# A routed-expert stage with one load queue split in two, and three smaller moves of order

## The chip, the cores and the metric

The kernel runs on one core of one Trainium2 chip. The metric is the device time of one execution in microseconds (us). Below, TensorE is the matrix engine (PE in the rows), VectorE is DVE, ScalarE is ACT, GpSimd is POOL and SyncE is SP; SP only waits and issues transfers.

## The reference, cut to what matters

Sixteen sequences of 64 rows (1024 rows in all, 512 wide) pass through three blocks, each added to its input:

```
x = x + cross_attention(layernorm(x), ctx)        # 16 heads, 1601 context rows per sequence
x = x + linear_attention(layernorm(x))            # elu + 1 feature maps, 16 heads
x = x + experts(layernorm(x))                     # 8 experts, each row goes to its best 2
experts: logits = x @ router.T; p = softmax(logits); two best experts of each row
         h = x @ w1[e].T (2048 wide); y = h[1024:] * silu(h[:1024]); out += p_e * (y @ w2[e].T)
```

## The kernel before, in words

All weights and activations that matter are held as two float32r parts: ScalarE rounds a tile to its high part, and VectorE or GpSimd subtracts to get the low part. A product is then three matmuls (high-high, high-low, low-high).

**The head.** The function `cross_attention` opens with the projections of the first sequence's context, `copy_unit` 0, 1, 2 and so on: TensorE fills one of two PSUM banks (L719), ScalarE copies it out (L617, L621). TensorE may fill a bank again when the copy of two units earlier is done. Units 0 to 3 make keys, units 4 and 5 are the first that need the value weights: for these ScalarE rounds `wv_hi` (L666) and VectorE subtracts `wv_lo` (L548). In the kernel before, ScalarE rounds `wv_hi` ahead of its copy of unit 0. ScalarE's square root before the copy of unit 6 (L674) waits for the variances of all rows of x.

**Linear attention and routing.** In `attend_route_and_experts` a loop over t works as a pipeline on tiles of 128 rows: at step t, tile t-1 makes its key-value blocks (KV, L1789), t-2 its heads (HEADS, L1811), t-3 is transposed (ATT_T, L1827), t-4 is projected (PROJ, L1836), then VectorE's `start_rows` (x, stats, mean, std: L1584, L902 to L904), a square root on ScalarE (L1393), VectorE's `finish_rows` (rstd, xn: L893, L894), the transpose of tile t-5 (TURN, L1848) and routing of tile t-6. Routing a tile is a chain: `route` on TensorE (logits, L1733), `choose` on VectorE (L1590 to L1600), `rank` on TensorE (L1745, L1747), `assign` on VectorE (L1606 to L1610), after which GpSimd scatters the tile's rows into `rows_in` (L1278). `route` of a tile waits for `assign` of the tile before it. Steps 8 to 13 have no new tile to start; there, `choose` and `assign` of tile t-6 stand at the end of VectorE's step and `rank` at the end of TensorE's. After them VectorE makes the tables (`slot_tables`, `combine_places`, `combine_weights`), in one row of small instructions.

**The experts.** `over_slots` runs a slot for each block of up to 384 rows of one expert, in order of falling counts: slots 0 to 6, written out, with WIDTH 384 (slots 0 to 4), 342 and 292 columns, then two kinds inside a loop that runs as often as the counts ask (not at all with these inputs) and a last slot of 256 columns. A slot has IT = 8 steps u. In step u TensorE does `up(s, u)` (24 matmuls, L1707), `down_part` of the slot before (9 matmuls, L1721) and in steps 3, 4 and 5 the transposes of one tile of the next slot's rows (`turn_rows`, 4 matmuls, L1691). The second and third `turn_rows` wait for VectorE's `rest_rows` (L1431) of the tile before, which follows ScalarE's `silu` (L1362), VectorE's product y (L1548) and ScalarE's `round_rows` (L1329) of the same step.

First-layer weights (w1) come in eight pieces of 512 KB a slot into RAW = 4 buffers. ScalarE's `split_w1` (L1309) and VectorE's (L1421) for piece u+2 (AHEAD = 2) stand in step u. Second-layer weights (w2) come in four pieces of 512 KB into two buffers; ScalarE's `split_w2` (L1316) of piece c stands in step 2(c+1), and GpSimd subtracts its low part (L1261), which frees the buffer. The last piece of a slot is split in step 0 of the next.

All these loads are issued by SP, in one order written by hand; a wait in it holds back everything behind it:

```python
for u in range(IT):
    ...                                   # slot 0, u == RAW: wait for the scatter, load_rows(0)
    if u == IT // 2 and not last:
        load_rows(s + 1)                  # the rows of the next slot, 768 KB
    sp.wait_ge(w1_lo_done, n - RAW + 1)   # then w1 piece u (L1235)
    if u % WC == WC - 1:
        sp.wait_ge(w2_lo_done, k - 1)     # then w2 piece u // 2 (L1242)
```

So the load of w2 piece 1 of a slot waits for GpSimd's work on the last piece of the slot before (step 0), piece 2 for step 2 and piece 3 for step 4, with the w1 pieces 4 to 7 standing behind them. ScalarE already issues one transfer a slot, `store_down` (L1339).

Of the kernel before, what the change touches and what calls it, by code (L numbers as in the profile page):

```python
# [118 lines left out]
def cross_attention(nc, ident, x, ctx, wq, bq, wk, wv, bk, bv, q_parts, attn_t, inv_t, rows_in, rows_out):  # L119
# [4 lines left out]
    with ExitStack() as mem:  # L124
# [480 lines left out]
        def _(act):  # L605
# [59 lines left out]
            act.wait_ge(wv_loaded, 16)  # L665
            nc.scalar.copy(wv_hi[:], wv_raw).then_inc(w_hi_done, 1)  # L666
            act.wait_ge(zeroed, 5)
            act.wait_ge(bias_loaded, 48)
            for kind, k in start_steps():
                if kind == "unit":  # L670
# [364 lines left out]
def attend_route_and_experts(nc, ident, m, rows_in, rows_out, w1, w2, out):  # L1035
# [4 lines left out]
    with ExitStack() as mem:  # L1040
# [142 lines left out]
        STEPS = TT + ROUTE  # L1183
# [26 lines left out]
        def _(sp):  # L1210
# [9 lines left out]
            def slot(s, par, last, width):  # L1220
# [3 lines left out]
                for u in range(IT):  # L1224
                    n = IT * s + u
                    if u == RAW and is_first(s):

                        sp.wait_ge(dispatched, 16 * 2 * TT)
                        sp.wait_ge(tables_done, 2)
                        load_rows(0)  # L1230
# [6 lines left out]
                    if u % WC == WC - 1:  # L1237
                        c = u // WC
                        k = NW2 * s + c
                        if positive(k - 1):  # L1240
                            sp.wait_ge(w2_lo_done, k - 1)
                        sp.dma_start(w2_raw[c % 2][:], w2[bass.ds(e, 1), c].rearrange(  # L1242
                            "a p (k n) -> (a p) k n", k=WC)).then_inc(w2_loaded[c % 2], 16)
# [58 lines left out]
        def _(act):  # L1302
# [7 lines left out]

            def split_w2(s, c):

                act.wait_ge(w2_loaded[c % 2], 16 * (s * (NW2 // 2) + c // 2 + 1))
                if positive(s):
                    act.wait_ge(parts_done, IT * (s - 1) + WC * (c + 1))
                nc.scalar.copy(w2_hi[:, WC * c:WC * c + WC, :], w2_raw[c % 2][:]).then_inc(w2_hi_done, 1)  # L1316
# [25 lines left out]
            def slot(s, par, last, width):  # L1342
                first = is_first(s)
                for u in range(IT):
# [17 lines left out]
                    nc.scalar.activation(silu[u % 2][:, 0:width], ps_up[u % 2][:, 0, 0:width], ACT.Silu).then_inc(silu_done, 1)  # L1362
                    if TURN_ROWS < u <= TURN_ROWS + RB and not last:
                        round_rows(s + 1, 1 - par, u - TURN_ROWS - 1)
# [45 lines left out]
        def _(dve):  # L1410
# [202 lines left out]
            for t in range(STEPS):  # L1613
                if 0 <= t - TURN < TT:
                    finish_rows(nc, dve, m, t - TURN, then, norm_sems)
                if ROUTE <= t < TT:
                    choose(t - ROUTE)
                r = t - KV
# [26 lines left out]
                if ROUTE <= t < TT:  # L1645
                    assign(t - ROUTE)
                r = t - PROJ
                if 0 <= r < TT:
                    start_rows(nc, dve, m, r, ready, then, norm_sems)
                if t >= TT:  # L1650
                    choose(t - ROUTE)
                    assign(t - ROUTE)
# [22 lines left out]
        def _(pe):  # L1675
# [95 lines left out]
            for t in range(STEPS):  # L1771
# [47 lines left out]
                if 0 <= r < TT:  # L1819
# [9 lines left out]
                    last.then_inc(att_turned, 1)  # L1829
                r = t - PROJ  # L1830
# [8 lines left out]
                if t >= TT:  # L1839
# [11 lines left out]
                if t >= TT:  # L1851
                    rank(t)
# [51 lines left out]
```

## Time and profile before

| | |
|---|---|
| three runs | 2516.23, 2516.41, 2518.18 us (median 2516.41) |
| the profiled execution | 2518.01 us, of which the profile's span is 2516.3 us |
| granted TensorE clock, mean | 0.974 |
| busy, TensorE / VectorE / ScalarE / GpSimd | 94% / 52% / 43% / 43% |
| cross attention | from 0 to about 1850 us, TensorE busy nearly throughout |
| linear attention and routing | about 1894 to 2060 us |
| experts, eight slots | 2078 to about 2491 us |
| gather, weighing, output | to 2516.3 us |

A row of the timeline gives start, duration, engine, line, operation, the tiles written and read, the count, and in square brackets the engine's idle time just before and who ended it. The chain of waits is the path followed back from the last instruction; its rows give start, duration and what ran or was waited for.

### The profile page before, as it was taken

Reading aid. Unit: us, or ns where it says so; the run is one execution under the profiler, and the core shown is the slowest. Engines: PE = TensorE matmul, PEld = TensorE weight load, DVE = VectorE, ACT = ScalarE, POOL = GpSimd, SP = SyncE. Lnnn points to the kernel's source line nnn. Section 1 sums busy time; section 2 is a strip of 40 time slices with the busy share of each in tenths; the row PEclk is TensorE's granted clock in tenths of the full one; section 3 lists DMA queues with packets and bytes.
Section 4 is the critical chain, followed back from the end, with each engine's and each line's share of the span. In section 5 each row is a group of like instructions: output and inputs, shape, how many; then the busy total and the mean of one; then the engine's idle time right before and its main releaser. Section 6 shows DMA issues by size and latency. Waiting matters only on the chain. (4 is left out here: it accounts for less than half of the span.)

```text
span 2516.3 us, 41241 instructions
## 1 busy us (share of the span) xinstructions
PE 2366.8 (94%) x14585; PEld 2092.1 (83%) x14585; DVE 1296.1 (52%) x2185; ACT 1086.3 (43%) x1865; POOL 1076.6 (43%) x439
## 2 busy tenths in 40 slices
PE   8999999999999999999999999999658958999985
PEld 7798998889899889989988998988527738999875
DVE  3245555555455555555545555555654465555544
ACT  3354544445444444444545454544412214444432
POOL 2255555555555555555555555555520021111114
PEclk9999999999999999999999999999879979999998
DMA  4311121221112121111212111123040034444444
GB/s 154 104 41 47 45 60 41 62 56 41 48 45 59 41 65 52 41 48 45 65 37 70 47 41 48 45 74 99 7 159 1 18 113 143 151 151 151 141 149 155
DMA packets 150050, 186.13 MB, mean 74 GB/s; under 512 B 79552, under 2 KB 108224, under 8 KB 149824
## 3 DMA queue, kind: packets, MB, share of 16 engines
q1 hardware_dynamic: 144192, 168.76, 21.7%
q0 software_dynamic: 2560, 8.39, 1.0%
q10 hardware_dynamic: 3072, 6.03, 0.6%
q8 instruction: 134, 2.20, 0.4%
q14 instruction: 92, 0.75, 0.2%
HBM read 139.29 MB, written 43.84 MB: 73 GB/s over the span
## 5 line engine op out<-in xcount | busy, mean ns | idle before, releaser
L399 POOL TENSOR_TENSOR k_parts<-k_t,k_parts 64x1602 fp32r<-64x1602 f32 x128 | 426.1, 3329 | 448.9 <-DVE k_parts L464 448.8
L719 PE MATMUL ps_kv<-ctx_hi,wk_hi 128*128 128x256 f32 (+1 forms) x1536 | 463.3, 302 | 9.1 <-DVE ctx_lo L578 7.6
L719 PE MATMUL ps_kv<-ctx_lo,wk_hi 128*128 128x256 f32 (+1 forms) x1536 | 441.2, 287 | 0.0
L719 PE MATMUL ps_kv<-ctx_hi,wk_lo 128*128 128x256 f32 (+1 forms) x1536 | 441.1, 287 | 0.0
L510 DVE TENSOR_TENSOR probs_t<-ps_pt,probs_t 128x512 fp32r<-128x512 f32 x368 | 205.9, 559 | 445.9 <-ACT probs_t L629 443.6
L413 POOL TENSOR_TENSOR v_parts<-v,v_parts 128x832 fp32r<-128x832 f32 x128 | 283.3, 2213 | 335.3 <-ACT v_parts L647 333.8
L719 PE MATMUL ps_kv<-wv_hi,ctx_hi 128*128 128x512 f32 (+1 forms) x832 | 340.9, 410 | 0.0
L719 PE MATMUL ps_kv<-wv_hi,ctx_lo 128*128 128x512 f32 (+1 forms) x832 | 327.9, 394 | 0.0
L719 PE MATMUL ps_kv<-wv_lo,ctx_hi 128*128 128x512 f32 (+1 forms) x832 | 327.1, 393 | 0.0
L617 ACT ACTIVATE k_t<-ps_kv,bk_sb 128x256 f32<-128x256 f32 (+1 forms) x384 | 185.6, 484 | 310.9 <-PE ps_kv L719 307.5
L719 PEld LDWEIGHTS ps_kv<-ctx_hi,wk_hi 128*128 128x128 f32 x1536 | 292.0, 190 | 12.5 <-issue 10.0
L719 PEld LDWEIGHTS ps_kv<-ctx_lo,wk_hi 128*128 128x128 f32 x1536 | 292.2, 190 | 1.9 <-issue 1.2
L719 PEld LDWEIGHTS ps_kv<-ctx_hi,wk_lo 128*128 128x128 f32 x1536 | 290.5, 189 | 0.0
L637 ACT ACTIVATE probs_both<-ps_s,neg_max 128x1601 f32<-128x1601 f32 x128 | 204.9, 1601 | 194.1 <-DVE neg_max L496 194.1
L388 POOL TENSOR_TENSOR ctx_lo<-ctx_raw,ctx_hi 128x1024 fp32r<-128x1024 f32 (+1 forms) x96 | 238.8, 2487 | 87.0 <-DVE ctx_hi L453 87.0
L494 DVE TENSOR_REDUCE row_max<-ps_s 128x1 f32<-128x1601 f32 x128 | 233.6, 1825 | 26.9 <-PE ps_s L733 19.3
L629 ACT CAST probs_t<-ps_pt 128x512 fp32r<-128x512 f32 x368 | 177.3, 482 | 161.4 <-PE ps_pt L765 152.2
L745 PEld LDWEIGHTS ps_o<-probs_t,v_parts 128*128 128x128 f32 (+1 forms) x1664 | 215.3, 191 | 30.1 <-DVE probs_t L510 20.0
L745 PE MATMUL ps_o<-probs_t,v_parts 128*128 128x256 f32 (+1 forms) x1664 | 220.4, 284 | 17.8 <-DVE probs_t L510 17.8
L621 ACT COPY v<-ps_kv 128x512 f32<-128x512 f32 (+1 forms) x208 | 120.7, 580 | 249.1 <-PE ps_kv L719 249.1
L1261 POOL TENSOR_TENSOR w_lo<-w_raw,w_hi 128x1024 fp32r<-128x1024 f32 x32 | 78.9, 2464 | 345.6 <-ACT w_hi L1316 345.6
L733 PE MATMUL ps_s<-k_parts,q_blocks 128*128 128x512 f32 (+2 forms) x1024 | 218.4, 356 | 2.0 <-issue 1.3
(275 smaller groups left out, 4113.4 us busy)
## 6 DMA issues: line engine op xcount, KB each, us to landing
w_raw<-w_dram SPq DMA_DIRECT2D x96, 512.0 KB, 4.9
ctx_raw<-ctx_dram SPq DMA_DIRECT2D x81, 512.0 KB, 3.9
rows_in<-zeros SPq DMA_DIRECT2D x150, 128.0 KB, 3.6
ctx_raw<-ctx_dram SPq DMA_DIRECT2D x16, 644.0 KB, 5.6
q_blocks<-q_parts SPq DMA_DIRECT2D x256, 32.0 KB, 1.9
rows<-rows_in SPq DMA_DIRECT2D x8, 768.0 KB, 6.2
rows_out<-zeros SPq DMA_DIRECT2D x1, 5376.0 KB, 17.7
rows_out<-down ACTq DMA_DIRECT2D x7, 768.0 KB, 3.6
```

Of the source, the lines that this page charges most:

```text
L388: nc.gpsimd.tensor_tensor(ctx_lo[c % 2][:, 0:w], ctx_raw[c % 2][:, 0:w], ctx_hi[c % 2][:, 0:w].bitcast(F32), ALU.subtract).then_inc(ctx_lo ...
L399: nc.gpsimd.tensor_tensor(k_parts[64 - 64 * s:128 - 64 * s, :], k_t[par][64 * s:64 * s + 64, g, :], k_parts[64 * s:64 * s + 64, :].bitcast ...
L413: nc.gpsimd.tensor_tensor(v_parts[:, :, 1, :], v[par][:, :, 64 * p:64 * p + 64], v_parts[:, :, 0, :].bitcast(F32), ALU.subtract).then_inc( ...
L494: nc.vector.tensor_reduce(row_max[:, q:q + 1], ps_s[:, S0:S0 + LC], AX.X, ALU.max).then_inc(max_done, 1)
L510: nc.vector.tensor_tensor(probs_t[0:m, j:j + k, 1, :], ps_turned[kv][g][0:m, 0:k, :], probs_t[0:m, j:j + k, 0, :].bitcast(F32), ALU.subtra ...
L617: nc.scalar.activation(k_t[par][:, which, CW * c:CW * c + w], ps_kv[bank][:, 0:w], ACT.Identity, bias=bk_sb[:, which:which + 1]).then_inc( ...
L621: nc.scalar.copy(v[par][0:m, which, :], ps_kv[bank][0:m, :]).then_inc(kv_copied, 1)
L629: nc.scalar.copy(probs_t[0:m, j:j + k, 0, :], ps_turned[kv][g][0:m, 0:k, :]).then_inc(pt_hi_done, 1)
L637: nc.scalar.activation(probs[q], ps_s[:, S0:S0 + LC], ACT.Exp, bias=neg_max[:, q:q + 1], scale=SCALE, accum_out=row_sum[:, q:q + 1]).then_ ...
L719: last = nc.tensor.matmul(o, still, moving, start=(k == 0 and i == 0), stop=(k == DT - 1 and i == 2))
L733: last = nc.tensor.matmul(ps_s[:, c0:c1], q_blocks[half][:, p % 4, part, :], k_parts[:, c0 - S0:c1 - S0], start=(part == 0), stop=(part == 1))
L745: last = nc.tensor.matmul(ps_o[:, 0:2], v_parts[0:m, j, :, :].rearrange("p a b -> p (a b)"), probs_t[0:m, j, :, :], start=(j == 0), stop=( ...
```

## The change

Four edits. (1) The w2 loads leave SP's order and are issued by ScalarE, through a new function `load_w2`: piece 0 after `silu` of step 0, piece 1 after that of step 1, piece 2 after step 3, piece 3 after step 5, each with the same wait for GpSimd as before; ScalarE reads the slot's expert number from the table once a slot. (2) In slot 0 SP issues the load of the first rows, with its wait for the scatter, ahead of w1 piece 2 (u == AHEAD) instead of ahead of piece 4. (3) For tiles 2 to 7 `choose`, `rank` and `assign` move from the end of step t to step t+1: `choose` after `finish_rows`, `rank` ahead of PROJ, `assign` after the heads and ahead of `start_rows`; the loop gets one step more. (4) ScalarE copies units 0 and 1 out before it rounds the value weights.

```diff
-            act.wait_ge(wv_loaded, 16)
-            nc.scalar.copy(wv_hi[:], wv_raw).then_inc(w_hi_done, 1)
             act.wait_ge(zeroed, 5)
             act.wait_ge(bias_loaded, 48)
             for kind, k in start_steps():
+                if kind == "unit" and k == 2:
+                    act.wait_ge(wv_loaded, 16)
+                    nc.scalar.copy(wv_hi[:], wv_raw).then_inc(w_hi_done, 1)
...
-        STEPS = TT + ROUTE
+        STEPS = TT + ROUTE + 1
...
-                    if u == RAW and is_first(s):
+                    if u == AHEAD and is_first(s):
...
-                    if u % WC == WC - 1:
-                        c = u // WC
-                        k = NW2 * s + c
-                        if positive(k - 1):
-                            sp.wait_ge(w2_lo_done, k - 1)
-                        sp.dma_start(w2_raw[c % 2][:], w2[bass.ds(e, 1), c].rearrange(
-                            "a p (k n) -> (a p) k n", k=WC)).then_inc(w2_loaded[c % 2], 16)
...
+            def load_w2(s, e, c):
+
+                k = NW2 * s + c
+                if positive(k - 1):
+                    act.wait_ge(w2_lo_done, k - 1)
+                act.dma_start(w2_raw[c % 2][:], w2[bass.ds(e, 1), c].rearrange(
+                    "a p (k n) -> (a p) k n", k=WC)).then_inc(w2_loaded[c % 2], 16)
...
+                    if u == 0:
+                        if first:
+                            act.wait_ge(tables_done, 1)
+                        e = act.value_load(slot_expert[0:1, bass.ds(s, 1)], min_val=0, max_val=E - 1)
+                        load_w2(s, e, 0)
+                    if u % WC == WC - 1 and u // WC + 1 < NW2:
+                        load_w2(s, e, u // WC + 1)
...
+                if t > TT:
+                    choose(t - 1 - ROUTE)
...
+                elif t > TT:
+                    assign(t - 1 - ROUTE)
...
-                if t >= TT:
-                    choose(t - ROUTE)
-                    assign(t - ROUTE)
...
+                if t > TT:
+                    rank(t - 1)
                 r = t - PROJ
...
-                if t >= TT:
+                if TT <= t < TT + ROUTE:
                     route(t, TT)
...
-                if t >= TT:
-                    rank(t)
```

## Rows read from the trace of the kernel before

**Rows 1.** TensorE's waits, 2040 us to the end: us in total, times, longest.

```profile
PE ps_one L1691 <- DVE rows_lo L1431: 13.1, 6, 4.6
```

**Rows 2.** SP's waits from 2060 us; the landing times of its 64 w1 loads (L1235).

```profile
SPq L1242 <- POOL w_lo L1261: 327.0, 30, 17.2
```

```profile
DMA to landing us min/median/max: 3.1/5.6/8.7
```

**Rows 3.** The chain of waits, slots 5 and 6.

```profile
2369.37 0.44 PE ps_one L1691 x4
...
2375.67 3.79 PE ps_pair L1707 x24
2379.45 2.06 PE ps_one L1721 x9
...
2388.73 0.33 SPq L1242
...
2390.45 8.00 DMA w_raw<-w_dram
```

**Rows 4.** Timeline of ScalarE, slots 1 to 6: ends of slots, two steps.

```profile
2173.45 1.56 ACT L1337 COPY down<-ps_one 128x512 f32<-128x512 f32 x3 [1.59 <-PE ps_one L1721]
...
2278.11 1.56 ACT L1337 COPY down<-ps_one 128x512 f32<-128x512 f32 x3 [1.59 <-PE ps_one L1721]
...
2329.65 1.56 ACT L1337 COPY down<-ps_one 128x512 f32<-128x512 f32 x3 [1.59 <-PE ps_one L1721]
...
2381.53 1.57 ACT L1337 COPY down<-ps_one 128x512 f32<-128x512 f32 x3 [1.58 <-PE ps_one L1721]
...
2426.33 0.41 ACT L1362 ACTIVATE silu<-ps_pair 128x292 f32<-128x292 f32 x1 [2.20 <-PE ps_pair L1707]
...
2431.61 0.42 ACT L1362 ACTIVATE silu<-ps_pair 128x292 f32<-128x292 f32 x1 [2.70 <-PE ps_pair L1707]
...
2433.70 1.56 ACT L1337 COPY down<-ps_one 128x512 f32<-128x512 f32 x3 [1.67 <-PE ps_one L1721]
```

**Rows 5.** Timeline of TensorE in slot 0.

```profile
2104.80 0.66 PE L1691 MATMUL ps_one<-ident,rows 128*128 128x128 f32 x4 [3.32 <-DVE rows_lo L1431]
```

**Rows 6.** Start of the experts: SP's timeline, chain of waits, timeline of VectorE.

```profile
2060.70 0.89 SPq L1235 DMA_DIRECT2D w_raw<-w_dram  x2
```

```profile
2064.57 9.22 DMA rows<-rows_in
```

```profile
2074.43 0.19 DVE L1535 TENSOR_REDUCE weight<-cross 128x16 f32<-128x32 f32 x1
2075.61 0.69 DVE L1431 TENSOR_TENSOR rows_lo<-ps_one,rows_hi 128x512 fp32r<-128x512 f32 x1 [0.99 <-ACT rows_hi L1329]
```

**Rows 7.** Timeline of TensorE, then VectorE, routing steps 7 to 9.

```profile
2018.53 0.95 PE L1733 MATMUL ps_one<-router_sb,o_t 128*128 128x8 f32 x8
...
2021.87 0.24 PE L1745 MATMUL ps_one<-chosen,before 128*128 128x8 f32 x1 [1.89 <-DVE chosen L1597]
...
2024.20 3.60 PE L1836 MATMUL ps_one<-lwo_sb,att_t 128*128 128x512 f32 x8
```

```profile
2012.30 0.16 DVE L893 RECIPROCAL rstd<-std 128x1 f32<-128x1 f32 x1 [0.27 <-ACT std L1393]
2012.50 0.55 DVE L894 TENSOR_SCALAR xn<-x,mean_var,rstd 128x512 f32<-128x512 f32 x1
...
2020.41 0.15 DVE L904 TENSOR_SCALAR std<-mean_var 128x1 f32<-128x1 f32 x1
```

**Rows 8.** Timeline of the head, all engines.

```profile
11.59 1.90 ACT L666 CAST wv_hi<-probs_both 128x2048 fp32r<-128x2048 f32 x1 [2.13 <-DMA probs_both<-wv_dram]
...
13.52 2.29 DVE L548 TENSOR_TENSOR wv_lo<-probs_both,wv_hi 128x2048 fp32r<-128x2048 f32 x1 [3.33 <-ACT wv_hi L666]
...
14.01 0.36 PE L719 MATMUL ps_kv<-ctx_hi,wk_hi 128*128 128x256 f32 x1 [0.98 <-ACT k_t L617]
...
16.95 0.39 PE L719 MATMUL ps_kv<-wv_hi,ctx_hi 128*128 128x512 f32 x1
...
26.08 0.39 PE L719 MATMUL ps_kv<-ctx_hi,wk_hi 128*128 128x256 f32 x1 [0.58 <-ACT k_t L617]
```

## The prediction

> **What bounds the kernel now.** The page's part 2 shows TensorE busy nine tenths or more from the second slice to past 1850 us; no edit but the fourth touches anything before that, and the fourth stands in its first 30 us. So I read TensorE's waits in the last 480 us and, for the experts, what stands behind them. The largest repeated wait is for `rest_rows`, 13.1 us in six pieces [rows 1]. The reader is to see that this is not VectorE's own slowness: the chain of waits leads from it back through ScalarE's `split_w1` to a w1 load that took 8.00 us, and in front of that stands SP at L1242, the w2 load [rows 3]. SP's own waits say why: 327.0 us, 30 times, it stood at L1242 for GpSimd's low part, at worst 17.2 us [rows 2]. The w1 load behind it needed a buffer that had been free long before. So in the experts TensorE is bound by its own work in some slots and by late issue of w1 in others.
>
> How much that costs is read from the ends of slots [rows 4]. Slot 4 took 2329.65 - 2278.11 = 51.5 us, which is TensorE's own work and no stall. Slots 2 and 3, of the same width, took 104.66 us together: 1.6 us too long. Slot 5 (342 columns) took 51.9 us; its own work is eight steps of 3.79 + 2.06 us and three transposes of 0.44 us [rows 3], 48.1 us: 3.8 us too long. Slot 6 (292 columns) took 52.2 us; its undisturbed step is 2431.61 - 2426.33 = 5.28 us [rows 4], eight with the transposes make 43.6 us: 8.6 us too long. The narrower the slot, the more the fixed chain of w2 split, low part, load and landing binds. The sum is 14.0 us, slow matmuls after stalls among it.
>
> **w2 loads on ScalarE (edit 1).** SP loses four waits and four issues a slot. A w1 load then waits only for its buffer, freed two steps after a use that lies four steps before the next, so it has some four steps, 21 us in slot 6, against a landing of 8.7 us at worst [rows 2]. ScalarE gains four issues of 0.33 us if they cost what they cost SP [rows 3], and one read of the expert number. Queued behind each are the next `split_w1`, `split_w2`, `round_y` and `silu`; VectorE's y and TensorE's next-but-one `up` wait for `silu`. The bound from below is nothing (ScalarE idles 2.20 us or more ahead of these `silu` [rows 4]). From above I take 1 us an issue, register work and read included, on the one path where it counts: in step 4 `silu`, y and `rest_rows` follow the split chain, and `down_part` (2.06 us) covers just about that much. I put 0.5 us, in slot 6 alone. The waits that move with the loads are met: w2 piece 1 is issued after step 1, one step after the split it waits for, pieces 2 and 3 likewise. Slots 1 to 6: -14.0 + 0.5 = **-13.5 us**, bounds -14 and -7 (half is kept if ScalarE or the transfers become late in turn).
>
> Bandwidth: the first six loads and the rows, 3.9 MB, had landed 13.1 us after the first issue (2060.70, the rows at 2073.79 [rows 6]), 300 GB/s; a slot needs 7.9 MB in 43.6 us, 180 GB/s.
>
> Slot 0 has no `down_part` to cover `rest_rows`. Its stall of 3.32 us [rows 5] is partly such a one: from the end of `up`, `silu`, y and `rows_lo` need some 1.9 us whatever the loads do, and a low part on GpSimd in the same step adds more. I take **-1.0 us**; bounds 0, and -3 if the matmuls behind it stay fast.
>
> **Which rule speaks against it.** SP's issue is 0.33 us [rows 3] while its wait is up to 17.2 us [rows 2], so what is moved here is a wait. The Trainium skill ("DMA: Bandwidth & Descriptors", section "Issuing engines are not separate DMA queues") says that DMAs of all issuing engines run on the same 16 engines and interleave, and that a second issuer only saves the time to initiate. By that rule alone 32 issues of 0.33 us would leave SP, none of them on TensorE's path, and the sum would be that of the rival "no change" below.
>
> **First rows earlier (edit 2).** The rows took 9.22 us to land because six loads stood in front [rows 6]; with two in front I estimate some 4 to 5 us. TensorE and ScalarE can then turn and round them early, but `rest_rows` stands behind VectorE's tables, which run to 2074.6 (2074.43 + 0.19) [rows 6]. `rest_rows` now begins at 2075.61 and its three pieces are paced by ScalarE at 0.86 us; with the high parts waiting they go at about 0.6 us. So `up` of slot 0 starts 1.0 + 0.5 = **-1.5 us** earlier, not five. The w1 pieces 2 and 3 land later by the rows' share, some 3 us, hidden by the same tables. The bound from above is 0.
>
> **Rankings one step later (edit 3).** In step 8 of before, TensorE's projection ends at 2018.5; VectorE reaches std at 2020.41; `rank` comes at 2021.87 after an idle 1.89 us; heads and transpose follow and the next projection starts at 2024.20 [rows 7]. After the change the heads and transpose run while VectorE works, and only `rank` stands ahead of the projection. But `choose` now stands behind `finish_rows`, which waits 0.27 us for ScalarE's root and needs about 0.2 + 0.6 us more [rows 7], 1.1 us with gaps. `rank` comes at 2021.87 + 1.1 = 2023.0 and the projection at 2023.2: 1.0 us gained in step 9. Step 10 has a transpose alone to hide (its gain and the 1.1 us cancel), step 11 has nothing left to hide and pays 1.1 us, and so does the chain of the last three tiles, once, when `finish_rows` of tile 7 stands ahead of `choose` of tile 5. Later tiles chain as before. -1.0 + 0 + 1.1 + 1.1 = 1.2, with 0.2 us for the longer idle: **+1.4 us**. The tables, the scatter and all behind them move by this. Bounds: -2 (the projection of step 11 runs at the faster pace) and +3 (more of the small matmuls run slow).
>
> **Two copies ahead of the value weights (edit 4).** `wv_hi` runs 11.59 to 13.49 and holds back the copy for which TensorE waits at 14.01 [rows 8]. After, unit 2 follows unit 1, which ended 0.98 us before that, at about 12.9, some 1.1 us earlier. `wv_hi` then starts behind the copy of unit 1, about 13.35, `wv_lo` (2.29 us) ends at about 17.6 instead of 15.8, and unit 4, which needs it, starts there instead of at 16.95: 0.65 us later, with TensorE idle before it. What comes next late is already late: at 26.08 TensorE waits 0.58 us for a copy behind the root of the variances, and VectorE's part of that chain starts after 18.1 in either kernel. So **+0.1 us**; bounds 0, and +2 if the idle 1.9 us slows the matmuls behind it.
>
> **The sum.** 0.1 + 1.4 - 1.5 - 1.0 - 13.5 = -14.5 us. Against the profiled execution (span 2516.3, time 2518.0) that is 2503.5; this execution lies 1.6 us above the median of the runs, 2516.4, and against the median it is 2502. The last slot, gather and output are unchanged and move along: their first instructions wait for the slot before, not for a load.
>
> **Rivals.** *Half the stalls stay.* ScalarE issues w2 piece 0 after `silu` of step 0 and splits it two steps on; if w2 lands late beside w1, or ScalarE's added work delays y in the turning steps, 7 us are kept: 2516.4 - 7 - 1 = 2509. For it: w1 landings of up to 8.7 us with one queue [rows 2]. Against: a step and more of slack on `silu`. *No change.* If lateness were the transfers' own and not the issue's, edits 2 and 3 cancel and the time is 2516 to 2517. For it: 8.00 us for one load, and the rule above. Against: that load had the 768 KB of rows in front of it and was issued behind SP's wait. *Slower.* One mechanism: w2 piece 0 blocks ScalarE. `silu` of step 2 is late from a landing of about 8 us in slot 6, and TensorE is late from about 12 us, since `up` needs the y of two steps before. Beyond that each us costs 7 slots 7 us. With 14 us of old stall given back first, it turns into a loss of over 5 us from a landing of about 15 us: 2516.4 - 14.5 + 7 x 3 = 2523. Nothing in the rows has such a landing.
>
> **How the numbers follow.** What a measurement of this kernel can tell from no change is about 0.2%, 5 us. Forecast 0.66, half 0.13, no change 0.12, slower 0.09. Faster is the first two, 0.79. With all terms at the favourable bound the time is 2516.4 - 14 - 3 - 1.5 - 2 = 2496, with all at the other 2516.4 - 7 + 3 + 2 = 2514; the range 2496 to 2511 holds the forecast and the half case and leaves the rest out. Alone, the forecast's own range is 2497 to 2508.
>
> **What would show it.** SP's wait at w2 is gone, and its w1 loads wait for VectorE's low parts. Ends of slots 1 to 6 are 51.5 us apart (four), 48 and 44. ScalarE's idle time ahead of `split_w1` for a DMA vanishes from slot 1 on. `up` of slot 0 starts within 1 us of 2078, the row load landing near 2070. TensorE's projection of step 9 starts 1 us earlier and the last `rank` 1.4 us later. Unit 4 starts at 17.6 and unit 8 still at 26.1. The prediction is wrong if ScalarE shows waits for w2 ahead of `split_w2` that reach `silu`, if slot 6 stays above 48 us, or if the routing gains or loses more than 3 us.

## The result, and the profile after

The changed kernel took 2510.15 us, median of 11 runs (2508.07 to 2513.64), beside 2517.69 us for the kernel before on the same chip: ratio 0.9969, 95% interval [0.996, 0.9978], or 7.5 us less. Forecast were 14.5 us less. The profiled execution has a span of 2509.2 us at a mean clock of 0.975 (before: 2516.3 and 0.974).

SP's waits from 2060 us, and the landing of its w1 loads, which answer to [rows 2]:

```profile
SPq L1236 <- DVE w_lo L1430: 278.0, 51, 14.3
```

```profile
DMA to landing us min/median/max: 3.1/3.4/8.0
```

The wait for GpSimd's low part is gone. Once the experts run, SP waits only for the w1 buffers and, before it loads rows, for TensorE's transposes (41.5 us in seven pieces). The median landing is 3.4 us, not 5.6. ScalarE's timeline at the ends of slots 1 to 6, which answers to [rows 4]:

```profile
2179.99 1.56 ACT L1339 COPY down<-ps_one 128x512 f32<-128x512 f32 x3 [1.59 <-PE ps_one L1731]
...
2282.92 1.56 ACT L1339 COPY down<-ps_one 128x512 f32<-128x512 f32 x3 [1.59 <-PE ps_one L1731]
...
2334.42 1.56 ACT L1339 COPY down<-ps_one 128x512 f32<-128x512 f32 x3 [1.59 <-PE ps_one L1731]
...
2382.50 1.57 ACT L1339 COPY down<-ps_one 128x512 f32<-128x512 f32 x3 [1.58 <-PE ps_one L1731]
...
2426.12 1.56 ACT L1339 COPY down<-ps_one 128x512 f32<-128x512 f32 x3 [1.67 <-PE ps_one L1731]
```

The slots last 51.5, 48.1 and 43.6 us, to a tenth what the prediction worked out as TensorE's own work. From the first of these rows to the last it is 246.1 us, where [rows 4] gives 260.2. That alone is -14.1 us, and the whole kernel gained 7.5: about as much was lost elsewhere. TensorE's waits from 2040 us [rows 1], then its timeline in slot 0 [rows 5]:

```profile
PE ps_one L1755 <- DVE chosen L1606: 6.3, 3, 2.9
PE ps_one L1701 <- DVE rows_lo L1440: 4.0, 2, 2.1
```

```profile
2087.16 0.66 PE L1717 MATMUL ps_pair<-rows_hi,w_hi 128*128 128x384 f32 x1 [4.56 <-DVE rows_lo L1440]
2112.77 0.66 PE L1701 MATMUL ps_one<-ident,rows 128*128 128x128 f32 x4 [2.09 <-DVE rows_lo L1440]
```

The waits for `rows_lo` in the experts are down from 13.1 us in six pieces to 4.0 in two, both in slot 0. But `up` of slot 0 begins at 2087.16, not near 2078. The routing explains part: two of its waits for `chosen` are 2.9 us each. The rest lies before the linear attention, where no edit was thought to reach: the output projection of the cross attention starts at 1849.3 us, 7.1 us later than before (1842.2).

ScalarE's timeline of before and of after, behind the first of the six returns of the loop of the cross attention, shows what is new there:

```profile
445.76 0.59 ACT L629 CAST probs_t<-ps_pt 128x512 fp32r<-128x512 f32 x1 [2.32 <-issue]
446.25 0.89 ACT L647 CAST v_parts<-v 128x832 fp32r<-128x832 f32 x1
```

```profile
446.08 0.59 ACT L629 CAST probs_t<-ps_pt 128x512 fp32r<-128x512 f32 x1 [2.28 <-issue]
448.26 0.89 ACT L647 CAST v_parts<-v 128x832 fp32r<-128x832 f32 x1 [1.60 <-issue]
```

"issue" means that nothing the profile shows was waited for. In the changed kernel this second stall stands at each of the six returns, and in the kernel before at none. ScalarE's waits over 110 to 1840 us, of after:

```profile
ACT v_parts L647 <- issue: 8.9, 6, 1.7
ACT probs_t L629 <- issue: 6.8, 3, 2.3
```

Behind `v_parts` stand ScalarE's next casts of `probs_t`, behind these VectorE's low parts and TensorE, whose wait "ps_pt <- DVE probs_t" grew from 4.2 us to 7.4. And ScalarE's program begins with an instruction that it had not before, at 0.11 us:

```profile
0.11 0.02 ACT L1907 BASE_LOAD   x1
```

It stands in the profiles with edit 1 and in none without: there ScalarE reads an expert number and addresses w2 by it. The packed traces also hold ScalarE's register and branch instructions, and there two register moves follow it: the branch of the first return is behind 562 instructions of ScalarE in the kernel before and behind 565 in the changed one. This gave theory F: the loop now stands later in ScalarE's program, so that the border between two pieces of program that are fetched one after the other falls behind the loop's first cast, and each return pays for two fetches in a row.

### The profile page after: what moved, and what is told of

It is laid out like the page before. It is cut to its first block and busy times, and to the rows that moved or that the text cites. A ratio compares the mean times of both kernels' runs of the same rounds, so it can differ in the third digit from the quotient of the medians.

```text
span 2509.2 us, 41269 instructions
## 1 busy us (share of the span) xinstructions
PE 2363.8 (94%) x14585; PEld 2087.0 (83%) x14585; DVE 1294.5 (52%) x2185; ACT 1091.0 (43%) x1866; POOL 1072.9 (43%) x439
## 5 line engine op out<-in xcount | busy, mean ns | idle before, releaser
L617 ACT ACTIVATE k_t<-ps_kv,bk_sb 128x256 f32<-128x256 f32 (+1 forms) x384 | 186.1, 485 | 308.6 <-PE ps_kv L720 305.9
L720 PEld LDWEIGHTS ps_kv<-ctx_hi,wk_hi 128*128 128x128 f32 x1536 | 292.2, 190 | 10.7 <-issue 8.6
L629 ACT CAST probs_t<-ps_pt 128x512 fp32r<-128x512 f32 x368 | 177.5, 482 | 162.3 <-PE ps_pt L766 155.5
```

What stands on the lines that cost most here:

```text
L617: nc.scalar.activation(k_t[par][:, which, CW * c:CW * c + w], ps_kv[bank][:, 0:w], ACT.Identity, bias=bk_sb[:, which:which + 1]).then_inc( ...
L629: nc.scalar.copy(probs_t[0:m, j:j + k, 0, :], ps_turned[kv][g][0:m, 0:k, :]).then_inc(pt_hi_done, 1)
L720: last = nc.tensor.matmul(o, still, moving, start=(k == 0 and i == 0), stop=(k == DT - 1 and i == 2))
```

## The experiments

Stretches of all the profiles, in us: A from the first store of `inv_t` (L304) to the first matmul of the output projection; B from the first product of the map that makes the values of the linear attention (`lwv_hi`, L1680 before), which the expectations call the first linear-map product, to the totals behind the last rank; C from there to the first `up`; D from the end of slot 1 to that of slot 6. "+n" is the number of added ScalarE instructions, and "at" the number of ScalarE's instructions ahead of the branch of the first return, counted in the packed trace. Ratios are to the kernel before on the same chip. A, B, C and D are from one profiled execution each, the medians from 4 to 12.

| label | edits | at | A | B | C | D | median us | ratio |
|---|---|---|---|---|---|---|---|---|
| before | none | 562 | 1636.7 | 118.0 | 21.0 | 260.2 | | |
| e1 | 4 | 562 | 1640.3 | 118.0 | 20.7 | 255.4 | 2516.82 | 1.0001 [0.9992, 1.0011] |
| e2 | 3 | 562 | 1640.2 | 120.5 | 20.7 | 257.2 | 2519.75 | 1.0012 [1.0, 1.0025] |
| e6 | none, +1 | 563 | 1641.8 | 118.1 | 20.9 | 258.2 | 2521.21 | 1.0004 [0.9993, 1.0015] |
| e8 | 2 | 562 | 1644.2 | 117.8 | 19.5 | 257.6 | 2518.83 | 0.9997 [0.9984, 1.0011] |
| e19 | none, +8 | 570 | 1639.1 | 118.0 | 20.5 | 258.2 | 2514.34 | 0.9977 [0.9966, 0.9988] |
| after | all | 565 | 1643.4 | 122.3 | 19.4 | 246.1 | 2510.15 | 0.9969 [0.996, 0.9978] |
| e14 | all, again | 565 | 1647.5 | 120.4 | 19.4 | 246.3 | 2513.54 | 0.9973 [0.9963, 0.9983] |
| e3 | 1, 2 | 565 | 1646.4 | 117.8 | 19.4 | 246.2 | 2511.53 | 0.9983 [0.9973, 0.9992] |
| e4 | 1, 2, 3 | 565 | 1644.1 | 120.5 | 19.4 | 246.3 | 2512.48 | 0.9985 [0.9976, 0.9993] |
| e12 | 1 | 565 | 1647.5 | 117.8 | 19.4 | 246.2 | 2508.03 | 0.9948 [0.9934, 0.9961] |
| e13 | all, two casts made one | 565 | 1647.0 | 120.5 | 19.4 | 246.2 | 2512.29 | 0.9965 [0.9952, 0.9978] |
| e7 | all, +4 | 569 | 1650.7 | 120.5 | 19.4 | 246.1 | 2516.52 | 0.9984 [0.9973, 0.9995] |
| e9 | 1, 2, 4, +4 | 569 | 1647.7 | 118.0 | 19.4 | 246.2 | 2513.40 | 0.9976 [0.9966, 0.9985] |
| e10 | all, +8 | 573 | 1641.5 | 120.0 | 19.5 | 246.2 | 2503.81 | 0.9931 [0.9918, 0.9945] |
| e15 | all, +8, again | 573 | 1637.9 | 122.2 | 19.4 | 246.2 | 2504.45 | 0.9933 [0.9919, 0.9947] |
| e11 | all, +16 | 581 | 1640.8 | 122.3 | 19.4 | 246.5 | 2506.99 | 0.9943 [0.993, 0.9956] |
| e16 | 1, 2, 4, +8 | 573 | 1635.0 | 117.8 | 19.5 | 246.2 | 2499.89 | 0.9926 [0.9912, 0.994] |
| e17 | 1, +8 | 573 | 1633.0 | 118.1 | 19.4 | 246.2 | 2497.45 | 0.9909 [0.9893, 0.9924] |
| e18 | all, +8, choose first | 573 | 1633.1 | 112.9 | 19.4 | 246.2 | 2497.70 | 0.9914 [0.99, 0.9929] |

**Edit 4 alone (e1)** and **edit 3 alone (e2).**

```diff
-            act.wait_ge(wv_loaded, 16)
-            nc.scalar.copy(wv_hi[:], wv_raw).then_inc(w_hi_done, 1)
...
+                if kind == "unit" and k == 2:
+                    act.wait_ge(wv_loaded, 16)
+                    nc.scalar.copy(wv_hi[:], wv_raw).then_inc(w_hi_done, 1)
```

> The kernel before with edit 4 alone (the copies of units 0 and 1 ahead of the value weights). Theory A, edit 4 costs the missing 6 us in cross attention by shifting its loop: time +6 us (ratio 1.0024), first matmul of the linear maps 6 us later than in the kernel before. Theory B, that shift is scatter between executions: ratio 1.0000 within 0.0006 (my +0.1 us), and the first matmul of the linear maps lies anywhere from 1893 to 1901. Either way unit 4 starts at 17.5 and unit 8 at 26.4.

```diff
-        STEPS = TT + ROUTE
+        STEPS = TT + ROUTE + 1
...
+                if t > TT:
+                    choose(t - 1 - ROUTE)
```

> The kernel before with edit 3 alone (rankings one step later). My prediction's term: +1.4 us, bounds -2 and +3. What the trace of the changed kernel suggests: the projections of steps 10 and 11 take 6.6 and 6.1 us instead of 4.4 and 5.3, tables 4.2 us later, so +4 us (ratio 1.0016). A rival, that the slow projections were scatter: +1.4 us or less.

Edit 4 measured nothing that can be told from zero, and the stall at L647 does not come with it. Edit 3 gave 1.0012, some 3 us, and its stretch B is 2.5 us longer than in the kernel before.

**Edits 1 and 2 (e3)** and **1, 2 and 3 (e4)**, with the head, or the head and the rankings, as before.

```diff
-                    if u == RAW and is_first(s):
+                    if u == AHEAD and is_first(s):
...
-                        sp.dma_start(w2_raw[c % 2][:], w2[bass.ds(e, 1), c].rearrange(
...
+                    if u % WC == WC - 1 and u // WC + 1 < NW2:
+                        load_w2(s, e, u // WC + 1)
```

> Edits 1 and 2 alone (w2 loads on ScalarE, first rows ahead of w1 piece 2). By my terms -13.5 -1.0 -1.5 = -16 us; by the trace of the changed kernel -14.1 (slots 1 to 6) -2.5 (slot 0) -1.6 (first up) + 0.5 (tail) = -17.7 us, ratio 0.9930. If something in these two edits costs the missing 6 us instead (theory C), -11 us, ratio 0.9955.

> The changed kernel without edit 4. Theory A (edit 4 costs 6 us in cross attention): -13.5 us against the kernel before, ratio 0.9946. Theory B (scatter) and C (another edit): the same as the changed kernel, ratio 0.997.

e3 misses its forecast by 13 us and that of theory C by 7, and e4 misses that of theory A by 10, although D is what it should be. Both have the stall at L647 six times (9.5 and 9.0 us), which e1 and e2 lack: it comes with edit 1 or edit 2.

**One instruction more in the kernel before (e6); four more in the changed one (e7).** A cast of `v_parts` in batch 0, ahead of the loop, is cut in two for each instruction wanted; the work is the same.

```diff
-                nc.scalar.copy(v_parts[:, :, 0, :], v[par][:, :, 64 * p:64 * p + 64]).then_inc(v_hi_done, 1)
+                if isinstance(b, int) and b == 0 and 1 <= p <= 1:          # <= 4 in e7 and e9
+                    nc.scalar.copy(v_parts[:, 0:6, 0, :], v[par][:, 0:6, 64 * p:64 * p + 64])
+                    nc.scalar.copy(v_parts[:, 6:JT, 0, :], v[par][:, 6:JT, 64 * p:64 * p + 64]).then_inc(v_hi_done, 1)
```

> The kernel before, with one ScalarE cast ahead of the cross attention's loop cut in two (the copy into v_parts of batch 0, pair 1, in pieces of 6 and 7 tiles), so that ScalarE's stream of the loop stands one instruction later, as it does in the changed kernel, where a register instruction now leads ScalarE's stream. Nothing else is changed, and the expert stage not at all. Theory F (each of the six returns of the loop waits for ScalarE's next piece of program, and where that piece begins decides which instruction is late): the v_parts cast that follows a return, L647, which in three profiles without the queue edit never waited and in three with it waited 1.3 to 1.9 us at every one of six returns with nothing released (issue), now waits so here too; TensorE's waits for probs_t at the returns grow by 0.5 to 1 us each, the output projection starts some 3 to 6 us later than in kernels of the old ScalarE stream, and the time is 3 to 6 us longer than before, ratio 1.001 to 1.0025. Rival S (the start of the output projection merely scatters from execution to execution, 1842 to 1855 us): no such idle time at L647, ratio 0.9995 to 1.0005. Rival Q (the second queue's presence itself slows the loop): no idle at L647, ratio 1.000.

> The changed kernel, with four ScalarE casts ahead of the loop cut in two (batch 0, pairs 1 to 4), so that ScalarE's loop stands four instructions later and begins where the piece of program that is fetched second began, or just behind. Theory F: the idle time of 1.3 to 1.7 us at the v_parts cast after each return goes away, the waits of TensorE for probs_t at the returns shrink by 0.5 to 1 us each, and 3 to 6 us come back: 2504 to 2507 us where the changed kernel gave 2510, ratio to before 0.994 to 0.9955. Rival S: the same as the changed kernel, 0.9965 to 0.9975. Rival Q (the second queue): 0.997 too, and idle time of ScalarE at the returns stays. If the four instructions put the border elsewhere in the loop where an engine is tight, the stall moves to another line and the ratio stays near 0.997.

Neither came as expected, yet the stalls moved. ScalarE's waits in the loop, of e6, then of e7:

```profile
ACT k_t L617 <- issue: 4.4, 5, 1.0
```

```profile
ACT probs_t L629 <- issue: 24.0, 6, 4.9
```

e6 was meant to stand where the changed kernel does, but that is three instructions later. With one more instruction the stall shows at the instruction behind L647, five times, and not at L647 itself. Alone this says little: the kernel before has it there once (0.7 us), and e8, whose ScalarE program is that of the kernel before, three times (2.3 us). With four more on top of edit 1 it merged with the one at L629: 4.3 to 4.9 us at five returns, TensorE's wait for `probs_t` 10.7 us, and 0.9984. So with the loop at 562 and 563 the second stall is at L617, at 565 at L647 and at 569 at L629: it moves towards the loop's start as instructions are added ahead.

**Edit 2 alone (e8)** is the row load's one line of the diff of e3; **e9** is e7 with the rankings in their old place.

> The kernel before with edit 2 alone: the first rows' load ahead of the third weight load in slot 0, all loads still on SP. Prediction: 1.5 us less up to the first up-projection, nothing in slots 1 to 6, which keep their stalls of SP's order (255 to 260 us from the first slot's end to the seventh's); no idle time at L647 (ScalarE's stream is untouched); ratio 0.999 to 1.0. Rival: the rows, once ahead, hold up w1 and w2 pieces and the slot gives the 1.5 us back, ratio 1.000. If the cross attention is 3 to 6 us later here too, edit 2 and not ScalarE's stream is what moves it, and theory F falls.

> Edits 1, 2 and 4 with the old place of the rankings, and the four cut casts of the run before it: the candidate for the best version. Edit 3 alone measured 1.0012 [1.0, 1.0025], some 3 us. Theory F and the rankings' price together: 2 to 4 us under the run with all four edits and four more instructions, that is 2501 to 2505, ratio 0.9925 to 0.995. If edit 3 costs nothing beside the others, the two are equal within 1 us. From the first linear-map product to the totals some 118 us as without edit 3, not 121 to 122.

e8 has no idle time at L647 and C of 19.5: edit 2 gives its 1.5 us when alone, and does not touch ScalarE. But its output projection starts 8.3 us later than that of the kernel before (A is 7.5 us longer), and that was to be the end of theory F. What makes e8 late is not the stall: TensorE's wait for `probs_t` is 2.5 us, less than before. TensorE was busy 3.5 us longer in A and idle 3.8 us longer, none of it for `probs_t`, and no run tells why. So the length of A in one profile cannot decide on theory F, for or against; it rests on what follows. e9 misses its range for the reason of e7; its B is 118.0.

**Eight more (e10), sixteen more (e11), edit 1 alone (e12), one fewer (e13).** e10 and e11 cut the eight casts of batch 0 in two or three. e13 makes one cast of two, and the one that is left waits for both loads:

```diff
+                if g == 2:
+                    continue
-                dims = slice(g * P, (g + 1) * P)
+                dims = slice(g * P if g < 2 else 2 * P, (g + 1) * P)
+                if g == 3:
+                    act.wait_ge(wk_loaded[2], 16)
```

> The changed kernel with eight more ScalarE instructions ahead of the cross attention's loop (the v_parts casts of batch 0 cut in two). With four more, ScalarE's idle time at the six returns was not gone but had moved to the first cast of probs_t and joined the return's own: 24.0 us at L629, 4.9 at most, and TensorE's waits for probs_t rose from 7.4 to 10.7 us. Theory F, mended: the border between two pieces of ScalarE's program lies a fixed number of instructions from the start of the program; one more instruction ahead moves it one instruction earlier in the loop; with four more it still lay just behind the loop's first instructions. With eight more it lies ahead of the loop: one fetch at a return, not two. Idle time at L629 back to 2 to 2.5 us a return and none at L647; TensorE's waits for probs_t at 4 to 5 us; output projection 4 to 9 us earlier than in the run with four more (1857.5); time 2 to 6 us under that of the changed kernel, ratio 0.994 to 0.996. Rival (any added instruction ahead costs, wherever the border is): as with four more or worse, ratio 0.998, idle of 4 to 5 us at L629.

> The same with sixteen more instructions (cut in three). Theory F: as with eight more, since the loop again begins behind the border; ratio within 0.0008 of that run. If eight more do not reach behind the border and sixteen do, the single fetch of 2 to 2.5 us at L629 shows here alone, and so does the gain. Rival (any added instruction costs): worse than with eight more.

> Edit 1 alone on the kernel before. Theory F: idle time at L647 of 1.3 to 1.9 us at six returns (it comes with edit 1 and with no other), TensorE's waits for probs_t 7 to 9 us against 2.5 to 4.7; in the experts the ends of slots 1 to 4 51.5 us apart, then 48 and 44, 246.2 us in all against 255 to 260; ratio 0.998 to 0.999. If edit 1 alone has no idle time at L647, it is not this edit that moves ScalarE's stream, and theory F is wrong about the cause.

> The changed kernel with one ScalarE instruction fewer ahead of the loop (the third and fourth casts of wk_hi made one). Theory F: the border moves one instruction later in the loop, behind the v_parts cast L647, whose idle time of 1.3 to 1.7 us a return goes away or moves to L617, where the kernel with one more instruction than before had it (4.4 us in five returns); TensorE's waits for probs_t fall from 7.4 to 3 to 5 us; time 1 to 4 us under the changed kernel, ratio 0.9955 to 0.997. The head costs at most 0.5 us more. Rival (the idle time comes from the DMA ring or the registers that edit 1 gives ScalarE, wherever its instructions stand): idle time at L647 as in the changed kernel, ratio 0.997 to 0.998.

With eight more both stalls are gone, where one fetch a return was expected to stay. ScalarE's timeline of e10, behind the same return:

```profile
444.86 0.59 ACT L629 CAST probs_t<-ps_pt 128x512 fp32r<-128x512 f32 x1 [0.69 <-PE ps_pt L773]
```

All that is left of "issue" in ScalarE's loop is 1.1 us, once. With sixteen more, 4.8 us are back in two pieces, both at L629, and the ratio is 0.0012 from that of e10, not within 0.0008. TensorE's wait for `probs_t` is 0.0 and 0.4 us. e12 has the stall at L647 in full (8.4 us in six pieces), so edit 1 is what brings it.

e13 misses too, with 7.8 us at L647, but it did not do what it was meant to. The packed trace has one wait on a semaphore in place of the cast that was taken out, so the branch is behind 565 instructions as in the changed kernel. It is the changed kernel once more, on this chip: eight more instructions are worth 2512.29 - 2503.81 = 8.5 us beside it, sixteen more 5.3 us. The rival named for it, that edit 1's own registers or ring bring the stall wherever the instructions stand, falls with e10, which has all of edit 1 and no stall.

**What the stalls are.** The page counts the packets that bring program to the engines (packets, MB, share of the DMA engines), on two queues. e10 differs from after in ScalarE's program alone. Of the pages of after, then of e10:

```profile
q14 instruction: 92, 0.75, 0.2%
```

```profile
q14 instruction: 63, 0.52, 0.1%
```

From 110 to 1840 us there are 73 on q14 in the kernel before, in the changed one and in every other kernel whose loop stands at 562, 563, 565, 569 or 581, and 43 in all six kernels at 570 and 573: 30 fewer at six returns. Those on q8 are 134 in all twenty profiles. And the stalls end with these transfers: in after two of q14 start at 444.27 and 446.55 us, and the two casts shown above that stood still start 1.81 and 1.71 us behind them. Of the 102 "issue" waits of ScalarE in that stretch of all profiles 94 end 1.4 to 2.1 us behind the start of such a transfer, and the other eight are of another kind (1.1 or 1.2 us, at places of their own). So the stalls are waits for program, and the place of the loop decides whether it is fetched anew at a return. Theory F had only the border wrong: the loop is 380 instructions long, and at 570 and 573 nothing at all is fetched, at 581 it is again. Why those places and not the others, no run shows.

**Side by side on one chip (e14 to e17)**: the changed kernel again, with eight more again, without edit 3, and edit 1 alone with eight more. The diffs are those above.

> The changed kernel once more, as the measure for the other three on the same chip. 0.9965 to 0.998. Six idle times at L647, 8 to 9 us in all; from the first inv_t store to the output projection 1643 to 1648 us, five or six of which theory F puts down to the returns.

> The changed kernel with the eight added ScalarE instructions once more. Theory F: no idle time at L647, TensorE's waits for probs_t under 1 us, 1640 to 1642 us from the first inv_t store to the output projection, and a time 4 to 7 us under the changed kernel's beside it, ratio to before 0.994 to 0.9955. Rival (the 0.9931 of the first time was that chip's and that call's scatter): within 2 us of the changed kernel.

> Edits 1, 2 and 4 with the eight added instructions, the rankings in their old place. If edit 3 costs what its own run gave (1.0012, and 120.5 us instead of 118 from the first linear-map product to the totals), this one is 2 to 4 us under the run with all four edits: ratio 0.9925 to 0.9945, the fastest of all. If edit 3 is neutral beside the others: equal within 1 us.

> Edit 1 alone with the eight added instructions. By the terms of the prediction it lacks edit 2's gain of 1.5 us and slot 0's half: 1 to 3 us over the run without edit 3. If edit 2 takes something back that the profile hides (edit 1 alone had 0.9948, edits 1 and 2 together 0.9983, on different chips), it is the fastest instead, by 3 us or more.

The eight instructions are worth 2513.54 - 2504.45 = 9.1 us, more than the 4 to 7 expected, as e13 and e10 have it on another chip; A differs by 9.6 us in the two profiles. Leaving out edit 3 gives 4.6 us more, with intervals that overlap. And edit 1 alone is not behind e16 but level with it or ahead: 2497.45 against 2499.89, intervals overlapping. That also leaves the 0.9983 of edits 1 and 2 (e3) and the 0.9948 of edit 1 (e12), each on its own chip, unexplained: their profiles have the same span, 2508.8 us.

**choose first (e18), and the kernel before with eight more (e19).**

```diff
+                if t > TT:
+                    choose(t - 1 - ROUTE)
                 if 0 <= t - TURN < TT:
                     finish_rows(nc, dve, m, t - TURN, then, norm_sems)
                 if ROUTE <= t < TT:
                     choose(t - ROUTE)
-                if t > TT:
-                    choose(t - 1 - ROUTE)
```

> All four edits and the eight added ScalarE instructions, and from step 9 on choose stands ahead of finish_rows on VectorE. If the prediction's reason holds (rank is late because choose waits behind finish_rows and its root, and TensorE's clock falls in the wait), TensorE's waits before the rankings of steps 10 and 11 shrink from 2.9 us by about 1, the projections of those steps run in 4 to 5.5 us instead of 6.1 to 6.7, and the stretch from the first linear-map product to the totals falls from 120 to 122.3 us to 117 to 119: time 1 to 4 us under the run with all four and eight more (2504.45 beside a before of 2519.22, 0.9933), ratio 0.992 to 0.993. If finish_rows is what TensorE's router product waits for, the wait only moves: the stretch stays at 120 or more and the ratio at 0.993.

> The kernel before with the same eight added ScalarE instructions. Theory F: the five kernels with the old ScalarE stream had 1636.7 to 1644.2 us from the first inv_t store to the output projection (1640.6 on average) with small waits for probs_t (2.5 to 4.7 us), the five with edit 1 and eight or sixteen more 1633.0 to 1641.5 (1637.6) with none. So the fetch at the returns costs the kernel before something too, about 3 us: TensorE's waits for probs_t under 1 us, ratio 0.998 to 0.9995. If it helps edit 1's stream alone: ratio 0.9995 to 1.0005 and the waits stay. The experts keep their 255 to 260 us.

TensorE's timeline in steps 9 to 11, of after and of e18:

```profile
2037.63 6.74 PE L1848 MATMUL ps_one<-lwo_sb,att_t 128*128 128x512 f32 x8
2048.55 0.34 PE L1755 MATMUL ps_one<-chosen,before 128*128 128x8 f32 x1 [2.90 <-DVE chosen L1606]
2048.97 6.19 PE L1848 MATMUL ps_one<-lwo_sb,att_t 128*128 128x512 f32 x8
```

```profile
2032.09 0.24 PE L1762 MATMUL ps_one<-chosen,before 128*128 128x8 f32 x1 [1.89 <-DVE chosen L1613]
2032.31 3.68 PE L1855 MATMUL ps_one<-lwo_sb,att_t 128*128 128x512 f32 x8
```

The wait is 1.0 us shorter, as expected, and both projections take 3.68 us in place of 6.74 and 6.19. B is 112.9 us, 9.4 less than in after and 5.1 less than in the kernel before, where 117 to 119 were expected. In the time it is less: 0.9914 beside the 0.9933 of the same kernel without this (e15), some 5 us, on two chips and with intervals that overlap. A window of after shows the clock in that stretch (PE busy, granted clock, DMA share, GB/s):

```profile
2040.00:2050.00 10.00, 7.10 (x22) 0.67 0.14 52
```

Granted 0.67 means that TensorE spent most of that window at 1.2 GHz, the lower of its two levels. In narrower windows the clock is 1.00 to 2036.3, 0.50 from 2037.2 to 2043, 1.00 again from 2044 to 2047 and 0.50 from 2048 to 2054. So the slow projection at 2037.63 does not stand behind a wait of 2.9 us: TensorE had just idled for 1.39 us and, one transpose later, for 0.90. The second stands behind the 2.90 us. In e18 the 0.90 us are gone and the 2.90 are 1.89, and the clock stays at 1.00 from 2010 to 2040 us. A wait of 1.89 us alone settles nothing, though: in the kernel before three such waits, one after another, are followed by projections of 3.60, 4.59 and 5.38 us.

e19 gained some 6 us (0.9977): the fetch at the returns cost the kernel before as well, at L629 (9.3 us in four pieces, 1.1 in e19), without a change to its work. That is more than the 0.998 to 0.9995 expected.

## Why the prediction was wrong, and what of it held

**What failed.** The step is the first, "no edit but the fourth touches anything before that", with which everything ahead of 1850 us was put at nothing. Edit 1 touches ScalarE's program, and with it where the loop of the cross attention lies in it. In A, six profiles with edit 1 and no instructions added give 1643.4 to 1647.5, mean 1646.0; the five of the kernel before, e1, e2, e6 and e8 give 1636.7 to 1644.2, mean 1640.6: **+5.4 us** that the sum had no term for. With edit 1 and eight or sixteen more the mean of six is 1636.9. A scatters by 4 us either way, so the single profiles prove little. What proves it is that the stall at L647 stands in all six profiles of the one kind and in none of the others, and the 9.1 us measured side by side. TensorE's wait for `probs_t` goes the same way: 3.8 us on average in the five, 7.7 in the six, 10.8 in the two with four more, 0.1 with eight or sixteen more. The size is less sure. The kernel before also fetches at its returns, and by the times eight more instructions gave it 0.9977, some 6 us, and the changed one 9.1: by that the new stall costs some 3 us, by A 5.4.

That the stalls are program being fetched is what the transfers on q14 show. The Trainium skill ("Runtime: NRT & Kernel Launch", section "Instruction fetch mechanics") says that program comes in blocks of 256 instructions and that a taken branch to a block no longer held forces a fetch before execution goes on. The trace agrees that a return can bring such fetches and that ScalarE stands still for them. The packets on q14 are smaller than the 16 KiB that the page gives for a block: 0.75 MB in 92, 8.2 KB each, beside 16.4 KB each on q8.

**Edit 1 in the experts.** Right in mechanism, a little large in size. D is 246.1 to 246.5 us in all 14 profiles with edit 1. Without it there are six, from 255.4 to 260.2, mean 257.8, and the profile from which I read 14.0 us of stall was the worst of them. The term is -11.6 us on average, not -13.5. It was also read from slots 2 to 6 alone, though it is called that of slots 1 to 6, and only three of the five slots behind the end of slot 1 last 51.5 us, not four. The rule of the Trainium skill ("DMA: Bandwidth & Descriptors", section "Issuing engines are not separate DMA queues"), that a second issuer only saves the time to initiate, would have had 0, and the trace does not agree: issues in one order share each other's waits, here 327.0 us of them [rows 2]. ScalarE issues at 0.34 us and never waited for w2.

**Slot 0 and edit 2.** The gain to the first `up` is there, 20.8 to 19.4 us (-1.4, forecast -1.5). But it does not need edit 2: edit 1 alone has 19.4 too (e12, e17). With two w2 loads off SP four loads stand ahead of the rows and not six. Edit 2 adds nothing beside edit 1, which the sum overlooked. Slots 0 and 1 gave 2.3 us (94.8 us on average without edit 1, 92.5 in after and e14, from the first `up` to the end of slot 1), slot 0's share being forecast at 1.0.

**Edit 3.** Forecast +1.4 us, within -2 and +3; B is longer by 3.0 on average (nine profiles of 120.0 to 122.3, ten of 117.8 to 118.1). In after it is 4.3, past the 3 us by which the prediction was to be called wrong. The reason given, `choose` behind `finish_rows`, is right: the projection of step 9 starts 1.1 us earlier as forecast, and e18 takes the cause away. What was undersized is "0.2 us for the longer idle". The last two projections took 10.0 us together in the kernel before (9.7 to 10.1 in the ten without edit 3), 10.5 to 10.8 in six profiles with edit 3 and 12.7 to 12.9 in three, after among them. Why the clock falls for longer in some executions than in others, no run shows.

**Edit 4.** Unit 4 started at 17.54 and unit 8 at 26.36, against 17.6 and 26.1 forecast [rows 8]. Unit 8 is 0.3 us later than in the kernel before, not 0.1, and neither can be told from zero in e1.

The terms as measured, cross attention, edit 4, edit 3, edit 2's, slots 0 and 1, slots 2 to 6: 5.4 + 0.3 + 3.0 - 1.4 - 2.3 - 11.6 = -6.6 us. The last slot and the output took 83.1 and 83.8 us (after, e14) against 82.4 on average without edit 1, another +1.1 that I can't explain; -5.5 beside -7.5 and -5.7 in the two measurements. Of the rivals none was the case: the time of "half the stalls stay", 2509, came about with all the stalls gone. So it is luck that 2510.15 lies within the range of 2496 to 2511.

## What to carry to other kernels

Splitting one hand-ordered queue pays where one of its waits (not its issues) stands in front of loads whose buffers are free; read its worth from more than one profile. An edit to an engine moves its whole program, so look at the same engine's "issue" idle time behind every return of every loop, and at the count of "instruction" transfers, in both profiles. Try some more instructions ahead of a loop before judging an edit by 0.3%, and more than one number of them: here four made it worse, eight took all the fetches away, sixteen brought them back, though most behind other waits. In a chain with little TensorE work put the short producer of the next matmul ahead of everything else: in e18 two waits shorter by about 1 us each came with projections that were 5.6 us shorter. The two fastest versions, edit 1 with eight more instructions (2497.45 us, 0.9909) and all edits with eight more and `choose` first (2497.70 us, 0.9914), are 14 to 16 us faster than the changed kernel.

## What the runs showed of the hardware

The same instructions in the same loop differ by 9.1 us of 2510 by where they stand in one engine's program, on an engine that is busy 43% of the time. A return of ScalarE's loop (380 instructions) brought five transfers of 8.2 KB of program in most kernels and none where the loop stood eight instructions later; a cast that needed one started 1.4 to 2.1 us behind the transfer's start. With TensorE idle for 1.39 and 0.90 us, one transpose between them, the granted clock fell from 1.00 to 0.50 and the next eight matmuls took 6.74 us (5.1 to 6.7 us in the nine profiles with these two waits); with the 1.39 us alone it stayed at 1.00 and they took 3.68 us.
